# Self-attention and feed-forward of a perceiver layer: heads by token tile instead of by head group

## The reference

```python
x = x + xattn(layernorm(x), ctx_512)            # 16 heads, 4096 keys
x = x + attn(layernorm(x))                      # attn: norm again (ln_w, ln_b), QKV, rope on half
                                                # of each 32-channel head, softmax, W_out, + its input
x = x + ffn(layernorm(x))                       # silu(bitlinear(x,w1)) * bitlinear(x,w3), bitlinear w2
# bitlinear: x rounded to 8 bits by its row's maximum; w rounded to -1, 0, 1 by mean(|w|) of the matrix
```

## Time and profile before

| | |
|---|---|
| median of 3 runs | 559.03 us (558.92 to 559.9) |
| profiled execution | 558.04 us, span 556.2 us, mean granted clock 0.999 |
| projections and rotations, 465.6 to 491.4 us, busy | PE 24.36, DVE 16.66, ACT 21.61, POOL 14.86 us of 25.8 |
| head loop, 491.4 to 519.3 us, busy | PE 27.23, DVE 20.61, ACT 23.15, POOL 26.40 us of 27.9 |
| w_out, norm, quantisation, 519.3 to 536.8 us, busy | PE 15.94, DVE 15.91, ACT 4.97, POOL 0 us of 17.5 |
| feed-forward, 536.8 to 556.2 us, busy | PE 14.51, DVE 13.77, ACT 4.84, POOL 2.44 us of 19.4 |

### The profile page before, as it was taken

One profiled execution on the slowest core, in us unless ns is written; L12 is line 12 of the kernel. 1 busy time (PEld: TensorE's weight loads), 2 busy tenths in 40 slices (PEclk: granted clock), 3 DMA queues, 4 the chain that ended last, 5 costly groups with the idle time before them and its releaser, 6 DMA issues.

```text
span 556.2 us, 10024 instructions
## 1 busy us (share of the span) xinstructions
PE 524.0 (94%) x3803; PEld 349.9 (63%) x3803; DVE 470.2 (85%) x708; ACT 366.3 (66%) x447; POOL 159.8 (29%) x202
## 2 busy tenths in 40 slices
PE   7999978799999999999999999999997898999996
PEld 3776743366667666766666667667676685556443
DVE  3579996999899899999999999999996547576996
ACT  2144335887876887787787788688787344987342
POOL 2579965002212202202202202202000001699200
PEclk9999999999999999999999999999999999999999
DMA  8999088599999999999999999999999997600001
GB/s 313 346 351 336 35 134 247 86 190 213 200 193 201 199 194 205 211 212 204 202 207 194 204 204 195 196 211 196 203 204 181 214 413 296 293 1 1 1 0 39
DMA packets 287806, 107.41 MB, mean 193 GB/s; under 512 B 276896, under 2 KB 277920, under 8 KB 286368
## 3 DMA queue, kind: packets, MB, share of 16 engines
q1 hardware_dynamic: 287776, 107.01, 88.8%
HBM read 37.26 MB, written 0.52 MB: 68 GB/s over the span
## 4 chain that ended last, share of the span: by engine, by line
PE 59%; DVE 24%; ACT 5%; DMA 5%; issue 4%; POOL 1%; SPq 1%; DVEq 0%; ACTq 0%; POOLq 0%
PE ps L661 16%; PE ps L663 8%; PE ps L643 8%; PE ps L645 8%; PE ps L644 8%; DMA pT<-split 5%; DVE rows L1269 4%; DVE split L1251 3%; PE ps L692 2%; DVE qrot L1307 2%; DVE qrope L1301 2%; ACT junk L1060 2%; DVE KL L1289 2%; DVE qrot L1304 1%; PE ps L805 1%
## 5 line engine op out<-in xcount | busy, mean ns | idle before, releaser
L661 PE MATMUL ps<-pT,VH 128*128 128x256 f16 x1024 | 195.5, 273 | 3.2 <-DMA pT<-split 3.1
L663 PE MATMUL ps<-pT,VL 128*128 128x128 f16 x1024 | 182.2, 219 | 0.0
L1269 DVE TENSOR_SCALAR_CACHE_REDUCE rows<-ps,qback 128x1024 f32<-128x1024 f32 x128 | 163.5, 1280 | 16.1 <-PE ps L645 16.1
L1029 ACT ACTIVATE split<-rows,rz 128x2048 f16<-128x2048 f32 x64 | 124.8, 1994 | 68.1 <-DVE rz L1217 63.3
L1251 DVE SCALAR_TENSOR_TENSOR split<-rows,rz,split 128x2048 f16<-128x2048 f32 x64 | 150.2, 2348 | 1.3 <-issue 1.2
L661 PEld LDWEIGHTS ps<-pT,VH 128*128 128x128 f16 x1024 | 100.2, 98 | 43.7 <-DMA pT<-split 6.1
L1015 ACT ACTIVATE rows<-rows,negm 128x2048 f32<-128x2048 f32 x64 | 127.2, 1988 | 0.2 <-DVE negm L1274 0.2
L663 PEld LDWEIGHTS ps<-pT,VL 128*128 128x128 f16 x1024 | 100.2, 98 | 27.3
L525 POOL TENSOR_TENSOR ctx_c<-acc 128x128 f32<-128x128 f32 x32 | 25.3, 791 | 295.8 <-ACT acc L1004 295.8
L643 PE MATMUL ps<-KH,qcur 128*128 128x512 f16 x256 | 97.1, 379 | 3.3 <-DVE rows L1269 3.3
L644 PE MATMUL ps<-KL,qcur 128*128 128x512 f16 x256 | 97.0, 379 | 0.0
(11 more groups left out here) (175 smaller groups left out, 636.2 us busy)
## 6 DMA issues: line engine op xcount, KB each, us to landing
w_sb<-w SPq DMA_DIRECT2D x3, 2816.0 KB, 16.3
wq_sb<-wq SPq DMA_DIRECT2D x4, 1024.0 KB, 9.9
wo_sb<-wo SPq DMA_DIRECT2D x16, 256.0 KB, 4.6
wkcq_sb<-wkcq SPq DMA_DIRECT2D x4, 768.0 KB, 10.0
keys<-ctxT SPq DMA_DIRECT2D x8, 256.0 KB, 11.0
stage<-ctxT SPq DMA_DIRECT2D x16, 128.0 KB, 9.8
stage<-kcos SPq DMA_DIRECT2D x8, 256.0 KB, 9.9
stage<-ksin SPq DMA_DIRECT2D x8, 256.0 KB, 10.5
```

Of the source, the lines that this page charges most:

```text
L661: nc.tensor.matmul(bank(6 + r % 2, 0, 256), VH[:, 4 * b + k, :], p.rearrange("p x q -> p (x q)"), start=(b == 0 and k == 0), stop=False)
L663: last = nc.tensor.matmul(bank(6 + r % 2, 0, 128), VL[:, 4 * b + k, :], p[:, 0, :], start=False, stop=(b == 7 and k == 3))
L1029: nc.scalar.activation(split[:, split_slot(r, half), :, 0, :], rows[:, k, half * 2048:(half + 1) * 2048].rearrange("p (b k) -> p b k", k=1 ...
L1269: nc.vector.tensor_scalar(rows[:, k, c * 1024:(c + 1) * 1024], ps[:, score_bank(s) * 512:(score_bank(s) + 2) * 512], qback[:, r // 2:r // ...
```

## The change

The head loop's units become 4 heads of one token tile: units 0 to 3 are tile 0, units 4 to 7 tile 1. Scores, transposes and copies keep their sizes and counts per unit; `head_scores` of unit 0 waits for K's two transposed copies and Q's first, that of unit 4 for Q's second. The exponentials give the row sums by `accum_out`; DVE takes the reciprocals of 128x4 (`head_reciprocals`); per pair of units PE spreads them with 8 small products against the identity and then multiplies values, 16 matmuls of 128 columns (`head_products`), and DVE copies and multiplies (`context_out`). Tile 0's `w_out` products stand in PE's list of units 4 and 5, its norm in DVE's unit 6 (with a root of its own by three Newton steps instead of ACT's), its residual copy in ACT's unit 6, its quantisation in DVE's unit 7. Three output products of tile 1 stand ahead of the last `head_products`. K and V of tile 1 are projected before Q of tile 1; the second half of Q's projection follows the first scores; Q's rotation, transpose and copy stand in units 0 and 1. w1 is loaded first, in two halves, and summed ahead of ACT's first root (its last quarter behind it); its mean is taken between tile 0's norms and tile 1's, and POOL rounds it before it adds the residual sums. w1 is clipped before the loop, w3 in unit 3. Two of the three late `keep_busy` calls are gone. Some tiles (h2, azs, arz, ainv) lie elsewhere in SBUF.

The diff, cut; from PE's list on, only lines that stand after the change:

```diff
-    QKV_BANK = ((4, 2, 3), (5, 6, 3))
+    QKV_BANK = ((4, 2, 3), (5, 3, 7))
+    KT_BANK, QT_BANK, OUT_BANK = (0, 2), (1, 3), (3, 7)
     HPARTS = ((0, 6 * 128), (6 * 128, FF))
     ASCALE = float(DH) ** -0.5
     WPIECES = 8
-    UNITS = AH // 2
+    UNITS = TT * FG
+    GROUPS = UNITS // 2
...
             sp.wait_ge(av_done, 16 * XH)
+            for k in range(2):
+                half = slice(k * DK * FF // 2, (k + 1) * DK * FF // 2)
+                sp.dma_start(w1_sb[:, half], w1[:, half]).then_inc(w1_in[k], 16)
             sp.dma_start(wink_sb[:, :, :], w_k).then_inc(win_in, 16)
             sp.dma_start(winq_sb[:, :, :], w_q).then_inc(win_in, 16)
             sp.dma_start(winv_sb[:, :, :], w_v).then_inc(win_in, 16)
-            sp.dma_start(w1_sb[:, :], w1).then_inc(w1_in, 16)
...
             weight_round(0, w1_sb, w1b)
+            for t in range(TT):
+                residual_sum(t)
             weight_magic(1, w3_sb)
...
             tile_transposes(z1[:, 0, :], 0, zT_done)
+            weight_sum(0, bank(6, 0, 1))
             project(0, 0)
             pe.wait_ge(x1_done, TT)
             project(0, 1)
             pe.wait_ge(z_done, TT + 4)
             tile_transposes(z1[:, 1, :], 1, zT_done)
             project(0, 2)
             project(1, 0)
+            project(1, 2)
+            def natural_transposes(t, j):
+                pe.wait_ge(rot_done, 2 * t + j + 1)
+                tile_transposes(qkn[:, t, j, :], (KT_BANK, QT_BANK)[j][t], qkT_done)
+            natural_transposes(0, 0)
+            natural_transposes(0, 1)
             pe.wait_ge(wmean_done, 1)
+            weight_sum(1, bank(6, 0, 1))
+            natural_transposes(1, 0)
+            pe.wait_ge(v_copied, 1)
+            project(1, 1, range(DK // 2))
...
+            def head_products(p):
+                m = p % 2
+                if p == 0:
+                    pe.wait_ge(v_copied, 2)
+                wait(pe, cT_done, p)
+                pe.wait_ge(arz_done, 2 * p + 2)
+                for y in range(2):
+                    for a in range(HPG):
+                        slot = a % 2 * 2 + y
+                        nc.tensor.matmul(ps[a * DH:(a + 1) * DH, 2 * 512 + 256 + y * 128:2 * 512 + 384 + y * 128],
+                                         arz[:, 2 * p + a // 2, slot:slot + 1].broadcast_to([128, DH]), ident[:, :],
+                                         start=True, stop=True, tile_position=(0, a * DH))
+                for x in range(2):
+                    pe.wait_ge(pT_done[x], 2 * p + 2)
+                for y in range(2):
+                    for k in range(TT):
+                        for a in range(HPG):
+                            h = 4 * (2 * m + y) + a
+                            last = nc.tensor.matmul(ps[a * DH:(a + 1) * DH, 2 * 512 + y * 128:2 * 512 + (y + 1) * 128],
+                                                    v_sb[:, k, h * DH:(h + 1) * DH],
+                                                    pT[:, (2 * p + a // 2) % PT_UNITS * 2 + a % 2, y, k, :],
                                                     start=(k == 0), stop=(k == TT - 1), tile_position=(0, a * DH))
                 last.then_inc(aav_done, 1)
+            def output_residual(t):
+                if t == 0:
+                    pe.wait_ge(wout_in, 16)
+                    pe.wait_ge(wmean_done, 3)
+                pe.wait_ge(x2_done, t + 1)
+                nc.tensor.matmul(bank(OUT_BANK[t]), ident[:, :], x_sb[:, t, :], start=True, stop=False)
+            def attention_output(t, g):
+                pe.wait_ge(cT_done, 2 * t + g // 2 + 1)
+                last = nc.tensor.matmul(bank(OUT_BANK[t]), cT[:, g, t * 128:(t + 1) * 128], wout_sb[:, g, :],
+                                        start=False, stop=(g == FG - 1))
+                if g == FG - 1:
+                    last.then_inc(ao_done, 1)
...
             head_scores(0)
             head_scores(1)
+            project(1, 1, range(DK // 2, DK))
+            for u in range(UNITS):
+                head_transposes(u)
+                if u + 2 < UNITS:
+                    head_scores(u + 2)
+                if u == 3:
                     weight_sum(2, bank(3, 0, 1))
+                if u >= 2 and u % 2 == 0:
+                    head_products(u // 2 - 1)
+                if u == 1:
+                    natural_transposes(1, 1)
+                if u == FG:
+                    output_residual(0)
+                    attention_output(0, 0)
+                    attention_output(0, 1)
+                if u == FG + 1:
+                    attention_output(0, 2)
+                    attention_output(0, 3)
+            output_residual(1)
+            attention_output(1, 0)
+            attention_output(1, 1)
+            head_products(GROUPS - 1)
+            quantised_transposes(0)
+            attention_output(1, 2)
+            attention_output(1, 3)
...
-            keep_busy(10, 2)
-            quantised_transposes(0)
             for t in range(TT):
+                if t == 1:
+                    quantised_transposes(1)
...
+            for c in range(3):
+                abs_sum(0, c)
             root(3, slice(0, 1))
+            abs_sum(0, 3)
             root(4, slice(0, 1))
             scale_shift(0)
             root(5, slice(1, 2))
             root(6, slice(1, 2))
...
+            transposed_copies(0)
+            nc.scalar.activation(warm[:, 1:2], ones[:, 0:1], ACT.Exp).then_inc(warm_done, 1)
+            abs_sum(2, 1)
...
+            def exponentials(u):
+                act.wait_ge(anm_done, u + 1)
+                wait(act, apT_done, 2 * (u - 3))
+                for x in range(HPG):
+                    o = (4 + u % 2 * 2) * 512 + x * TOK
+                    nc.scalar.activation(prob[:, (u + 2) % 4, x, :], ps[:, o:o + TOK], ACT.Exp, bias=anm[:, u, x:x + 1],
+                                         accum_out=azs[:, u, x:x + 1]).then_inc(aexp_done, 1)
+            def probabilities_out(u):
+                wait(act, aav_done, (u - 1) // 2)
+                if u >= BOTH_FROM:
+                    act.wait_ge(apT_done, 2 * u + 1)
+                    nc.scalar.activation(pT[:, u % PT_UNITS * 2].rearrange("p y k t -> p (y k t)"), bank(0), ACT.Copy)\
+                        .then_inc(pT_done[0], 1)
+                act.wait_ge(apT_done, 2 * u + 2)
+                nc.scalar.activation(pT[:, u % PT_UNITS * 2 + 1].rearrange("p y k t -> p (y k t)"), bank(1), ACT.Copy)\
+                    .then_inc(pT_done[1], 1)
+            def residual_copy(t):
+                nc.scalar.activation(x_sb[:, t, :], bank(OUT_BANK[t]), ACT.Copy).then_inc(x3_done, 1)
+            exponentials(0)
             natural_copy(1, 1)
+            for u in range(UNITS):
+                if u + 1 < UNITS:
+                    exponentials(u + 1)
+                if u == 6:
+                    act.wait_ge(var_done, 3 * TT + 1)
+                    residual_copy(0)
+                probabilities_out(u)
+                if u < 2:
+                    abs_sum(2, 2 + u)
+                if u == 1:
+                    transposed_copies(1)
             act.wait_ge(h2T_ps, 1)
+            nc.scalar.activation(h2T[:, 0, :], bank(OUT_BANK[0]).bitcast(bf16)[:, 0:DM], ACT.Copy).then_inc(h2T_done, 1)
...
+                if own_root:
+                    link(nc.vector.tensor_scalar(rs[:, tiles].bitcast(i32), ve[:, tiles].bitcast(i32), -0.5, ROOT_SEED,
+                                                 ALU.mult, ALU.add))
+                else:
...
+                for _ in range(3 if own_root else 1):
...
+                if t == 1:
+                    weight_scale(0, bank(6, 0, 1))
                 layernorm(x_sb, h1, t, t + 1)
                 dve.wait_ge(z_done, TT + 2 * t + 1)
                 layernorm(h1, z1, t, t + 1)
+                if t == 0:
+                    weight_total(0)
...
+            def head_reciprocals(u):
+                dve.wait_ge(aexp_done, HPG * (u + 1))
+                nc.vector.reciprocal(arz[:, u], azs[:, u]).then_inc(arz_done, 1)
...
+            def context_out(p):
+                t, m = p // 2, p % 2
+                dve.wait_ge(aav_done, p + 1)
+                nc.vector.tensor_copy(ainv[:, :], bank(2, 256, 512)).then_inc(ainv_done, 1)
+                dve.wait_ge(ainv_done, p + 1)
+                nc.vector.tensor_tensor(cT[:, 2 * m:2 * m + 2, t * 128:(t + 1) * 128],
+                                        bank(2, 0, 256).rearrange("p (g t) -> p g t", g=2),
+                                        ainv[:, :].rearrange("p (g t) -> p g t", g=2), ALU.mult).then_inc(cT_done, 1)
...
+            def output_norm(t):
                 dve.wait_ge(ao_done, t + 1)
+                layernorm(x_sb, h2, t, t + 1, bank(OUT_BANK[t]), x3_done, own_root=t == 0)
+            def output_quantise(t):
                 dve.wait_ge(z_done, 3 * TT + t + 1)
                 quantise(h2[:, t, :], h2b[:, t, :], xdq[:, t:t + 1], t, h2b_done)
```

(98 more changed lines are left out.)

227 lines of the change are left out of this document (63 added, 164 removed).

## The result

The changed kernel took 565.14 us (median of 8 runs, 560.37 to 567.9) against 559.04 (8 runs, 558.25 to 559.9): ratio 1.0105, 95% interval 1.0066 to 1.0144. The forecast was 558.5, with 555.5 to 562.3 as its range. The profiled execution, the longest of the eight, spans 566.0 us, and its granted clock is 0.976 on the mean; before it was 0.999. The ratios to before leave out, as slow, one run of e2_gate (883.0 us, granted clock 0.571) and the four of e11_before_no_idle above 567 us, while the medians count them.

What follows compares the result with a forecast made beforehand. TensorE was taken to bound the head loop, with waits on ScalarE and VectorE around it. A loop start 3.0 us earlier, mostly given back, put the first hmid product at 536.35 against 536.82: 558.5 us, range 555.5 to 562.3.

Steps and rivals of the forecast that it cites:

- unit 0's scores: Start of the head loop: first scores at 488.4 us instead of 491.36, with shorter TensorE work ahead of them.
- units 0 to 3: Tile 0's head units, slowed by VectorE and ScalarE: 13.9 us for what TensorE could do in some 9.
- units 4 to 6: Head loop to the third products' end, bound by TensorE's list, five output products included: 17.55 us, to 519.85.
- the stall: TensorE stands 3.2 us before its last transposes, behind VectorE's context and statistics and ScalarE's residual and bank copies.
- from the last transposes to tile 1's statistics: Transposes, output products, last head products, context and two more output products, until statistics start at 531.15 us: 8.10 us.
- The tail: Feed-forward from the first hmid product to the end, hanging on VectorE's order alone and left as it is: 19.4 us.
- the price of a rotation beside GpSimd: VectorE's four rotation instructions while GpSimd works: 2.8 us, with 1.7 to 3.2 as bounds.
- Rival B: Slower: TensorE's clock falls in the wait before the last transposes, +2.5 us, 561.0 us; chance 0.20.
- tile 1's norms beside GpSimd's first pass: VectorE's norm steps for tile 1 beside GpSimd: some 0.3 us longer, mostly covered by TensorE's first two projections.
- D: Rival: the new load order is late for ScalarE's first root or the first projection by 2 to 3 us, 561; chance 0.05.
- C: Rival: halved columns don't halve a product step; a group takes 2.5 instead of 1.52 us, end at 562.4; chance 0.10.
- A: Rival: the mixed head loop hides more, with rotation clear of GpSimd, free row sums and cheaper products: 556.7 us; chance 0.25.

Runs made afterwards that it cites:

- e2_gate: Changed kernel, with GpSimd's rounding of the second weight starting only after all four rotations: 560.5 us, ratio 1.0028 to the kernel before.
- e11_before_no_idle: Kernel before, without the two runs of 9 and 10 idle products that the change removed: 563.0 us; ratio 1.0037 on the eight runs below 567 us.
- e5_gate_fill: Changed kernel with GpSimd's second rounding held until the rotations are done, plus 13 idle products before the last transposes: 560.0 us, ratio 1.0023 to the kernel before.
- e4_fill: Changed kernel, rotation left as it was, with 13 idle products in each of TensorE's two waits: 560.3 us, ratio 1.0021 to the kernel before.
- e6_gate_copy: Changed kernel with GpSimd's second rounding after the rotations and tile 0's residual copied after the last probabilities: 558.3 us, ratio 0.9988 to the kernel before.
- e8_order: Changed kernel with rounding after the rotations, later residual copy, new VectorE order, 6 and 4 idle products in TensorE's last two waits: 557.8 us, ratio 0.9978.

## Why the prediction was wrong

Against the forecast the changed kernel's stretch is 8.50 us longer. By the table's steps (measured minus forecast, each as a difference of neighbours): unit 0's scores +0.63, units 0 to 3 +3.71 (17.61 against 13.9), units 4 to 6 +2.85 (20.40 against 17.55; the clock is at half up to 515), the stall −0.17 (3.03 against 3.2), from the last transposes to tile 1's statistics +1.70 (9.80, from 531.88 to 541.68, against 8.10; the clock again), from there on −0.22. The cross-attention ends 1.81 later; its clock fell at 109 and 423 us, but the profile of e5_gate_fill, without a fall, has 1.11 of it too. The tail is the same, 19.34 against 19.4.

**Failed: the price of a rotation beside GpSimd.** "I take 2.8 wherever POOL works", with 1.7 to 3.2 as bounds. The rows behind it show VectorE taking turns with the pieces; the same instruction can also lose every turn. Measured 7.06 for the four instructions (495.92 to 502.98), and 3.47 where they took turns (e4_fill), above the bounds too. The gate alone takes the ratio from 1.0070 to 1.0028. The Trainium skill (SBUF — State Buffer, Who interferes with whom) gives the shared ports to whoever issues first for one whole instruction; the trace shows 6.19 us over eight instructions, so the measurement goes beyond the rule.

**Failed: the clock behind TensorE's waits, and the idle products that leave, at no price.** They were in the diff, and the sum has no term for them. e11_before_no_idle shows what they were worth in the kernel before: 2.5 us in the median of its eight quicker runs, 3.9 in that of all twelve. What the same two calls would be worth in the changed kernel, whose waits lie elsewhere, isn't shown. Rival B named the clock and the point from which it decides, rightly: 0.50 when the last transposes start. But it was priced at one stall of 2.5 us and 0.20; the clock also fell in the rotation's wait, which the forecast didn't have, and stayed down from 501 to 515 us. Idle products in all waits of the head loop bring the gated kernel from 1.0028 (1.0008–1.0047) to 0.9998 (0.9983–1.0013).

**Mis-sized: tile 1's norms beside GpSimd's first pass.** "Under PE's first two projections", but TensorE waited 0.83 us for z of tile 1 (its transposes started at 476.75), and the scores were 0.63 late. Both of tile 1's norms ran beside GpSimd's pass: the step that makes z took 0.98 instead of 0.55, and the six such steps of the two norms together 2.5 us more than alone, where the prediction's estimate was some 0.3.

**Right.** The order of loads: TensorE waited 0.52 us for the first projection's operand, 0.64 before, so D didn't occur. A group of products took 1.53 us (518.38 to 519.91 at clock 1.00) against 1.52, so C falls. The line through the Trainium skill's figures (TensorE: Matmul & The Clock Gate, Back-to-back issue gap) gave an estimate of 2.5; the measured 1.53 decides. The stall, its place and its releaser. The sum itself: where the rotation takes turns and the clock stays up, the stretch is 71.80 (e4_fill) instead of 71.50; where the gate keeps the rotation clear as well, 70.49 and 70.51, mostly by units 0 to 3 (12.74 instead of 13.9). That is A's direction, with the gate added. With gate and idle products the change brings 1.48 us in that stretch (71.97 − 70.49), of which the whole span keeps 0.4 (556.2 to 555.8) and the median nothing that can be measured.

**Slips of sums.** Some terms don't add up as written: by the shares that it names, "within" comes to 0.33 and "slower" to 0.32, not 0.36 and 0.28, and A with half a us more is 556.2, not 555.5. Neither touches the forecast.

**Open.** Why VectorE and GpSimd took turns in e4_fill and not in the changed kernel, with starts 0.04 and 0.06 us apart, and whether a gap or that moment let the rotation in; in how many executions the hold occurs, and so how much of the median is its own and how much the clock's; why the clock falls in a wait of 2.6 us in one execution and not in another; and the 1.1 us by which the cross-attention, untouched, ended later without a fall of the clock.

## What to carry to other kernels

Before moving a long pass of GpSimd, list VectorE's instructions that now lie beside it (here the rotation's, with two inputs, and the norm's scaling), and take the rest of the whole pass, not one piece, as the upper bound of each; a wait that puts the pass behind them is cheap if GpSimd has time (e2_gate). Idle products are part of a schedule: when a change removes some or opens waits on TensorE like the ones here, price the work behind them at half speed as one case. When the mean clock differs between runs, compare stretches of profiles whose clock is 1.00 with the forecast, and medians with the kernel before.

## What the hardware showed that was not expected

An unbroken row of eight pieces on GpSimd held one VectorE instruction for 6.19 us, while other rotation instructions beside such rows took at most 1.01; the three held ones began 0.06 to 0.08 us behind a piece's start, the others earlier or later. After waits of at most 1.1 us, several in a row, the granted clock fell to 0.50 (e6_gate_copy, e8_order). The kernel before, unchanged, spreads from 557.4 to 560.9 us, with mean clocks of 0.999 and 0.991 at the two ends.
